# Two-element products on VectorE: a pair-wise reduction in place of a multiply, in the softmax of a quantised attention

## The reference, cut to what matters

```
q, k, v = x @ wq, ctx @ wk, ctx @ wv                       # 16 heads, 512 x 512 scores per head
sim  = fq(q, dq) . fq(k, dk) * SCALE                       # fq rounds to 8-bit steps of size d
attn = softmax(sim)                                        # row max, exp, row sum
out  = fq(attn, dw) . fq(v, dv)                            # attn / dw is rounded, clipped at 255
```

## Time and profile before

| | us |
|---|---|
| median of 3 runs | 3207.56 (3205.08 to 3210.16) |
| the profiled execution's own time | 3203.77 |
| its span, first to last instruction | 3202.0 |
| outside the span (3203.77 − 3202.0) | 1.8 |

### The profile page before, as it was taken

How to read it: one execution, slowest core, us unless ns; L and a number is a source line. 1 busy time by engine, 2 the same in 40 slices (tenths; PEclk the granted TensorE clock), 3 DMA queues, 4 the chain that set the end, 5 groups by cost and what they waited for, 6 DMA issues and landing times. The chain is left out here.

```text
span 3202.0 us, 57992 instructions
## 1 busy us (share of the span) xinstructions
PE 2905.9 (91%) x19128; PEld 1688.7 (53%) x19128; DVE 2257.2 (70%) x5109; ACT 1960.0 (61%) x4167; POOL 1497.5 (47%) x2258
## 2 busy tenths in 40 slices
PE   5999989999999999899989999998889899999991
PEld 2445443544354445444543544354444459999991
DVE  3797797989798879978897989798856643111115
ACT  3676676765767676767676765766536354444442
POOL 4654482567266626644682667265714622111115
PEclk9999999999999999999999999998989899999996
DMA  4001321233132204220321222131143339999995
GB/s 112 24 11 47 99 64 53 66 74 90 34 91 72 69 22 106 56 76 27 113 73 43 69 71 77 34 100 53 53 156 91 117 115 329 327 326 326 325 329 162
DMA packets 264462, 358.82 MB, mean 112 GB/s; under 512 B 30558, under 2 KB 235486, under 8 KB 257808
## 3 DMA queue, kind: packets, MB, share of 16 engines
q1 hardware_dynamic: 254960, 336.97, 35.0%
q0 software_dynamic: 6480, 17.58, 1.5%
q10 hardware_dynamic: 2768, 1.06, 0.1%
HBM read 292.55 MB, written 64.86 MB: 112 GB/s over the span
## 5 line engine op out<-in xcount | busy, mean ns | idle before, releaser
L1645 ACT ACTIVATE quant<-ps,nbias,sc 128x512 f32<-128x512 f32 x1024 | 790.3, 778 | 266.9 <-DVE nbias L1496 202.3
L1263 POOL TENSOR_SCALAR quant<-quant,rstep 128x512 f16<-128x512 f32 x1024 | 714.2, 697 | 470.9 <-DVE rstep L1502 219.8
L1517 DVE TENSOR_REDUCE m<-ps 128x1 f32<-128x512 f32 (+3 forms) x1024 | 558.7, 582 | 219.4 <-PE ps L1811 139.0
L1493 DVE TENSOR_REDUCE nmax<-ps 128x2 f32<-128x1024 f32 x512 | 620.9, 1216 | 43.4 <-PE ps L1780 40.6
L2209 ACT ACTIVATE hT<-moe_ps,expert_b 128x128 f32<-128x128 f32 x568 | 207.6, 368 | 269.2 <-PE moe_ps L2123 231.0
L1811 PE MATMUL ps<-kst,qst 96*128 96x512 bf16 (+3 forms) x1024 | 322.8, 353 | 46.0 <-DVE m L1517 23.5
L1509 DVE TENSOR_SCALAR big<-ps 128x1024 bf16<-128x1024 f16 x512 | 347.8, 679 | 19.0 <-PE ps L1788 16.8
L1788 PE MATMUL ps<-id,quant 128*128 128x128 f16 x4096 | 321.5, 223 | 39.2 <-DVE big L1509 28.7
L1788 PEld LDWEIGHTS ps<-id,quant 128*128 128x128 f16 x4096 | 251.9, 99 | 194.4 <-issue 112.1
L1664 ACT ACTIVATE big<-ps 128x256 f32<-128x256 f32 (+1 forms) x608 | 251.1, 467 | 92.0 <-PE ps L1836 52.6
L2404 DVE COPY words<-plain_rows 128x3 uint32 x71 | 12.0, 169 | 417.8 <-PE moe_ps L2175 417.8
(11 more groups left out here) (292 smaller groups left out, 4953.8 us busy)
## 6 DMA issues: line engine op xcount, KB each, us to landing
e_w<-in_L_xattn_e_w_dram SPq DMA_DIRECT2D x70, 1024.0 KB, 7.5
quant<-in_L_xattn_e_w_dram SPq DMA_DIRECT2D x36, 1024.0 KB, 7.5
uT<-in_L_xattn_e_w_dram SPq DMA_DIRECT2D x36, 1024.0 KB, 6.9
wring<-in_L_xattn_ff_w_dram SPq DMA_DIRECT2D x96, 256.0 KB, 2.8
parts<-parts_sb SPq DMA_DIRECT2D x64, 384.0 KB, 2.9
qst<-parts SPq DMA_DIRECT2D x32, 768.0 KB, 5.7
kst<-parts SPq DMA_DIRECT2D x32, 384.0 KB, 4.7
plain_rows<-rows_in SPq DMA_DIRECT2D x71, 140.0 KB, 2.6
```

Of the source, the lines that this page charges most:

```text
L1263: nc.gpsimd.tensor_scalar(pq[:, u % 2, h, :], probs[:, u % 2, h, :], rstep[:, u % 2, h:h + 1], HALF_ROUND, ALU.mult, ALU.add).then_inc(SIG ...
L1493: nc.vector.tensor_reduce(nmax[:, n % 2, :], ps[:, a:a + 2, :], AX.X, ALU.max, negate=True).then_inc(SIG["M"], 1)
L1517: nc.vector.tensor_reduce(m32[:, g % 2, t, h:h + 1], bank(("A", B, s, n))[:, 0:width], AX.X, ALU.max, negate=True).then_inc(SIG["am"], 1)
L1645: nc.scalar.activation(probs[:, u % 2, h, :], ps[:, BANKS[("S", B, s, u)][h], :], ACT.Exp, bias=nbias[:, u % 2, h:h + 1], scale=sc[:, s:s ...
```

## The change

- nb becomes a `tensor_reduce` with mult. The tile `nmax` is now 128 x 2 x 6 floats: for each attention s, two columns for odd units, two for even ones, and two columns that hold `sc` for good. `beside` forms a view 128 x 2 x 2 in which each head's row maximum has the factor as its partner; the reduction multiplies the two. M writes into its place in this tile.
- RS becomes the same with a tile `rsum` of the same form, whose last two columns hold 1/dw for good. E writes the row sums there, R inverts them in place (the tile `rinv` is gone), and the reduction multiplies by the partner.
- Two copies at the start fill the columns that stay (`CONSTS` grows from 20 to 22), behind one more wait.
- `step_in` is no tile of its own any more but lies in `m32`, which is used later.

The order of the steps on every engine, their number and their waits are as before but for the two copies and their wait.

```diff
+RING_AT = (2, 0)
...
-        step_in = sb("step_in", [P, 8], F32)
...
-        nmax = sb("nmax", [P, 2, 2], F32)
+        nmax = sb("nmax_beside_scale", [P, 2, 6], F32)
         nbias = sb("nbias", [P, 2, 2], F32)
-        rsum = sb("rsum", [P, 2, 2], F32)
-        rinv = sb("rinv", [P, 2, 2], F32)
+        rsum = sb("rowsum_beside_step", [P, 2, 6], F32)
...
+        step_in = m32[:, 0, :, :].rearrange("p t h -> p (t h)")[:, 0:8]
...
+        def beside(tile, s, n):
+
+            return tile[:, s, RING_AT[n % 2]:6].rearrange("p (a h) -> p h a", h=2)[:, :, 0::2 if n % 2 else 1]
...
-        CONSTS = 20
+        CONSTS = 22
...
+            dve.wait_ge(s_set, 20)
+            nc.vector.tensor_copy(nmax[:, :, 4:6], sc[:, 0:2].unsqueeze(2).broadcast_to([P, 2, 2])).then_inc(s_set, 1)
+            nc.vector.tensor_copy(rsum[:, :, 4:6], inv_step[:, 3::4].unsqueeze(2).broadcast_to([P, 2, 2])).then_inc(s_set, 1)
             dve.wait_ge(s_set, CONSTS)
...
                 if kind == "M":
-                    nc.vector.tensor_reduce(nmax[:, n % 2, :], ps[:, a:a + 2, :], AX.X, ALU.max, negate=True).then_inc(SIG["M"], 1)
+                    nc.vector.tensor_reduce(nmax[:, s, RING_AT[n % 2]:RING_AT[n % 2] + 2], ps[:, a:a + 2, :], AX.X, ALU.max, negate=True).then_inc(SIG["M"], 1)
                 if kind == "nb":
                     after(dve, "M", B, s, n)
-                    nc.vector.tensor_scalar(nbias[:, n % 2, :], nmax[:, n % 2, :], sc[:, s:s + 1], None, ALU.mult).then_inc(SIG["nb"], 1)
+                    nc.vector.tensor_reduce(nbias[:, n % 2, :], beside(nmax, s, n), AX.X, ALU.mult).then_inc(SIG["nb"], 1)
                 if kind == "R":
                     after(dve, "E", B, s, 2 * n + 1)
-                    nc.vector.reciprocal(rinv[:, n % 2, :], rsum[:, n % 2, :]).then_inc(SIG["R"], 1)
+                    nc.vector.reciprocal(rsum[:, s, RING_AT[n % 2]:RING_AT[n % 2] + 2], rsum[:, s, RING_AT[n % 2]:RING_AT[n % 2] + 2]).then_inc(SIG["R"], 1)
                 if kind == "RS":
                     after(dve, "R", B, s, n)
-                    nc.vector.tensor_tensor(rstep[:, n % 2, :], rinv[:, n % 2, :], inv_step[:, 4 * s + 3:4 * s + 4].broadcast_to([P, 2]),
-                                            ALU.mult).then_inc(SIG["RS"], 1)
+                    nc.vector.tensor_reduce(rstep[:, n % 2, :], beside(rsum, s, n), AX.X, ALU.mult).then_inc(SIG["RS"], 1)
...
-                                         accum_out=rsum[:, u % 2, h:h + 1]).then_inc(SIG["E"], 1)
+                                         accum_out=rsum[:, s, RING_AT[u % 2] + h:RING_AT[u % 2] + h + 1]).then_inc(SIG["E"], 1)
```

## The result

The changed kernel takes 3155.5 us in the median of 3 runs (3149.0 to 3158.5) against 3207.6 before: 52 us less. The ratio is 0.9845, 95% interval 0.9831 to 0.9859, or 45 to 54 us. The profiled execution, the quickest of the three, took 3149.0 against 3203.8.

A forecast was written before the change was run, and what follows sets the result against it. TensorE (93% busy) and VectorE (86%) were nearly full, neither quite, in the stage with the units. A gain of 41 us and +0.4 at the start gave −40.6, so 3167 us; range 3148 to 3197.

The forecast's parts named there:

- The hold: nb and RS wait within their own duration for GpSimd's instruction; a reduction does not. Saves 215 ns per nb, 48 per RS.
- The price of the reduction: A mult reduction of 4 elements into two outputs, for nb and RS, taken at 157 ns, ends 140 and 186.
- VectorE's time: Sign in the profile after: VectorE busy about 133 us less, near 2124, if the forecast is right.
- Flat cost: Rival, chance 0.08: the reduction escapes the tail but nb still costs 229 ns; middle 29 us, so 3179.
- The sum: Total gain in the stage with the units, between 23 and 59 us; the middle, 41 us, was taken.
- upper bound: Places where ScalarE waited for nb (48.4 us) and GpSimd for RS (10.8 us) pass on the whole saving: 59 us.
- lower bound: By TensorE, the fullest engine: only the 108 times it was really idle for E count, 23 us, nothing for RS.
- The start: One more wait and two copies in front of everything: +0.2 to +0.5 us, taken as +0.4.
- VectorE is the bound: Rival, chance 0.07: every ns of VectorE counts; 133 us go, and if half arrived, 66 us: 3141.
- Late next: In the unit loop, a step no longer late uncovers the next: M waits for S, or Q for the transposes; unsized.
- Behind the units: The 319 us after the units and the 588 us of experts only start earlier or later and keep their length.

The follow-up runs named there:

- nb_tt: The changed kernel with nb as a tensor_tensor of two SBUF operands, RS still reduced: 0.9903 of the kernel before, a gain of 31 us.
- q_quarter_before: The kernel before the change with GpSimd's Q cut to 128 of 512 keys (but for the first two units): ratio 0.9871, a gain of 42 us.
- both_again: The changed kernel itself run once more, against the kernel before: ratio 0.9835, a gain of 53 us.
- padded runs: The changed kernel with nb reducing 80 or 216 elements in 384 of 512 units, never held: 0.9863 and 0.9891 of the kernel before.
- rs_alone: Only RS reduced, nb the tensor_scalar of the kernel before: ratio 0.9936 against that kernel, a gain of 21 us.

## Why the prediction was right, and where its numbers were off

The predicted 3167 us lie 11.5 us above the measured 3155.5, inside the range of 3148 to 3197. The direction is as forecast, and so is the mechanism of the hold. How the saving reaches the end of the program was not understood product by product, and that the sum came so close is in part luck. Point by point:

- **The hold.** nb and RS wait inside their own duration for GpSimd, and a reduction doesn't: shown by the maxima after (161 ns), by the ends of all long products (behind a GpSimd instruction), by `nb_tt` (held again, 1066) and by `q_quarter_before` (the mean follows Q's length).
- **The price of the reduction.** 157 ns was taken; 149 and 153 were measured, so the reductions of the earlier trace rows were a fair guide for one with mult.
- **VectorE's time.** "Near 2124" was said, 2138.7 us were measured, 118.5 less than before. The durations of the two products fell by 139 us, but the 133 us of the prediction were a sum of durations too, and those overlap with their neighbours'. The other groups of VectorE kept their times, so no hold moved to them. The last nb started at 2240.3, near the 2250 forecast.
- **Flat cost.** The rival, and the fixed term of the Trainium skill ("VectorE: DVE Perf Modes", TRN2 errata) by which it would be the same for every operation, is refuted: 229, 161 and 148 ns for the same two results as a tensor_scalar, tensor_tensor and reduction.
- **The sum.** The step that was mis-sized is "I take the middle, 41 us" between 23 and 59. The upper bound was almost reached (52, and 53 in `both_again`). The lower bound took TensorE's busy time for work. It isn't: with the same matmuls TensorE was busy 15 us less in the stage (11 us in `both_again`), beside the 33 us of idle time that went.
- **The split of the sum.** "Upper bound by the waits" gave nb 48 us and RS 11; measured are 29 to 31 and 20 to 24 (each alone, and with the other reduced). For nb, it let every waiting place pass its whole saving on. What came instead: E waited 73 us less for nb, but 35 us more for Q. For RS, it counted the places where GpSimd stood idle for RS, times the mean saving. But the saving sits in the 69 held RS, and while they are held GpSimd is busy with the very instruction that holds them. Their delay falls on what stands behind RS on VectorE; that this is where the missing 10 us lie is likely, and wasn't tried by itself. The two errors offset each other in the sum, which is the luck.
- **The start.** "+0.2 to +0.5 us, I take +0.4": from the last product of `sc` to the first statistics it was 0.20 us before (19.80 to 20.00) and 0.48 after (20.15 to 20.63), so +0.28. The small operations in front of it began another 0.35 us later (19.39 and 19.74); in `both_again` they began at 19.43, so this isn't the change.
- **VectorE is the bound.** Refuted as a whole: 139 us freed gave 52, 0.4 for each. The padded runs put the price of one more us of nb at some 0.2 us of the total after the change.
- **Late next.** "M then waits for S, or Q for the transposes": the first rose, from 39.9 to 62.7 us, which the prediction also named as a sign that it is wrong; it came, and yet the gain was larger than forecast. The second fell, from 190.7 to 173.1. Two that rose were not named: E for Q (+35 us, the most) and R for E (+22).
- **Behind the units.** "Keep their length" held for the experts. The last exact attentions were 6.5 us shorter in the profiled execution, at a higher granted clock (0.94 against 0.93).

## What to carry to other kernels

When an operation of a few elements has a mean far above its median, look in the timeline at what GpSimd is doing when it ends; if the ends coincide, try a form that was never held here, such as a reduction over pairs. Free every such operation of a run on the queue together, since the hold passes to the next one that can be held. And don't price a hold only by the idle time of the engine that waits for its result: that gave 48 us for nb, which brought about 30, and 11 for RS, which brought 20 to 24.

## What was not expected of the hardware

- The form of a two-element product sets its price: 229 ns with a per-partition scalar, 161 with a second tensor, 148 as a reduction of pairs. The one tensor_scalar of this size with a constant in place of the scalar (L1311) took 170.
- The hold moves: with nb freed, the unchanged RS went from 205 to 284 ns in the mean, and VectorE's time for it from 104.1 to 145.1 us. Of the total that cost some 3 us (53 − 29 − 21), which is inside the intervals.
- A us of VectorE time has no single price: nb's cost or brought a fifth to a third of a us, held or not; RS's in `rs_alone` brought more than half.
